# A graph network's gate pass: the next group's target columns and own products ahead of the present group's sums in TensorE's order

## The reference

```python
xs = x[src]
xd = x[dst]
att = jax.nn.sigmoid(xs @ W_att[:d] + xd @ W_att[d:] + b_att)
messages = (xs @ W_msg + b_msg) * att
aggregated = jax.ops.segment_sum(messages, dst, num_segments=num_nodes)
gi = aggregated @ W_ih.T + b_ih
gh = x @ W_hh.T + b_hh
```

## Time and profile before

| | |
|---|---|
| runs shown, median (lowest to highest) | 4062.01 us (4057.37 to 4065.38) |
| profiled execution | 4062.75 us |
| its span | 4060.9 us |
| TensorE matmul, weight load, busy | 3201.5 us (79%), 2287.2 us (56%) |
| VectorE, ScalarE, GpSimd, busy | 2351.6 (58%), 1235.2 (30%), 2712.1 us (67%) |
| TensorE's granted clock, mean over the span | 0.873 |

### The profile page before, as it was taken

How to read it: one execution, slowest core, us unless ns; L and a number is a source line. 1 busy time by engine, 2 the same in 40 slices (tenths; PEclk the granted TensorE clock), 3 DMA queues, 4 the chain that set the end, 5 groups by cost and what they waited for, 6 DMA issues and landing times. The chain is left out here.

```text
span 4060.9 us, 70549 instructions
## 1 busy us (share of the span) xinstructions
PE 3201.5 (79%) x23417; PEld 2287.2 (56%) x23529; DVE 2351.6 (58%) x7900; ACT 1235.2 (30%) x2830; POOL 2712.1 (67%) x2717
## 2 busy tenths in 40 slices
PE   4878888888778888835544449987999889997996
PEld 4766666766556565423322235545666666675554
DVE  6888888998656676666666752244233433333223
ACT  3433344445434454343322330003111221112112
POOL 4777777777527676457747747735777577774774
PEclk7999999999889998855555569998999999998998
DMA  5434445667825454123345469955999689996995
GB/s 153 118 83 105 108 112 113 140 128 147 187 88 138 126 142 121 33 65 79 83 95 105 89 150 294 295 174 187 305 300 300 202 274 303 304 301 204 296 294 183
DMA packets 529216, 702.83 MB, mean 173 GB/s; under 512 B 72345, under 2 KB 420648, under 8 KB 528084
## 3 DMA queue, kind: packets, MB, share of 16 engines
q1 hardware_dynamic: 421204, 436.31, 37.7%
q0 software_dynamic: 107648, 261.94, 23.5%
HBM read 579.27 MB, written 118.69 MB: 172 GB/s over the span
## 5 line engine op out<-in xcount | busy, mean ns | idle before, releaser
L1742 POOL DMA_INDIRECT pass_rows<-table_sage,src_idx x1040 | 1000.1, 962 | 352.4 <-issue 296.7
L1132 POOL DMA_INDIRECT first_rows<-table_tensor,src_idx x772 | 769.7, 997 | 248.4 <-issue 230.8
L1791 PE MATMUL pass_dense_ps<-x 128*128 128x512 f16 x3528 | 602.6, 327 | 30.2 <-DMA x<-table_sage 29.5
L2848 POOL DMA_INDIRECT sort_rows<-table_sort,slot_idx x392 | 398.1, 1016 | 170.6 <-issue 157.6
L1791 PE MATMUL pass_dense_ps<-rb 128*128 128x512 f16 x2646 | 466.3, 331 | 28.5 <-DMA rb<-table_sage 24.3
L1791 PEld LDWEIGHTS pass_dense_ps<-x 128*128 128x128 bf16 x3528 | 335.1, 98 | 242.6 <-DMA x<-table_sage 31.6
L1386 POOL DMA_INDIRECT pass_rows<-table_gate,src_idx x314 | 328.9, 1047 | 167.1 <-issue 90.5
L1791 PEld LDWEIGHTS pass_dense_ps<-rb 128*128 128x128 bf16 x2646 | 228.7, 98 | 234.7 <-DMA rb<-table_sage 23.8
L1870 DVE TENSOR_TENSOR pass_scaled_sums<-pass_sums_ps,rc 128x52 f32<-128x52 f32 (+16 forms) x316 | 56.9, 222 | 518.3 <-PE pass_sums_ps L1833 492.3
L1219 PE MATMUL pass_sums_ps<-pass_hot,pass_prod_a 128*128 128x128 f32 x1568 | 241.1, 301 | 142.2 <-DVE rb L1236 136.5
L1219 PEld LDWEIGHTS pass_sums_ps<-pass_hot,pass_prod_a 128*128 128x128 f32 x1568 | 208.5, 206 | 197.0 <-DVE rb L1236 182.0
(11 more groups left out here) (387 smaller groups left out, 6357.1 us busy)
## 6 DMA issues: line engine op xcount, KB each, us to landing
rb<-dense SPq DMA_DIRECT2D x196, 288.0 KB
x<-dense SPq DMA_DIRECT2D x294, 192.0 KB
x<-table_sage SPq DMA_DIRECT2D x294, 192.0 KB
rb<-dense SPq DMA_DIRECT2D x98, 309.5 KB
pass_counts<-dense SPq DMA_DIRECT2D x147, 192.0 KB
rb<-table_sage SPq DMA_DIRECT2D x294, 96.0 KB
dense<-re SPq DMA_DIRECT2D x49, 448.0 KB
dense<-x SPq DMA_DIRECT2D x42, 448.0 KB
```

Source lines behind the costliest of these rows:

```text
L1132: nc.gpsimd.indirect_dma_start(rows[:, h, t, :], None, table, bass.IndirectOffsetOnAxis(ap=idx[:, at:at + 1], axis=0)).then_inc(gathered[h ...
L1742: nc.gpsimd.indirect_dma_start(rows[:, h, t, :], None, table, bass.IndirectOffsetOnAxis(ap=idx[:, at:at + 1], axis=0)).then_inc(gathered[h ...
L1791: ins = nc.tensor.matmul(dense_ps[:, a * bank_cols + at:a * bank_cols + to], table_ring[:, k, from_table:from_table + P], counts_ring[:, k ...
L2848: nc.gpsimd.indirect_dma_start(rows[:, b, j, :], None, table, bass.IndirectOffsetOnAxis(ap=slot_idx[:, at:at + 1], axis=0)).then_inc(gathe ...
```

## The change

Target columns and own products of a group become a function, `columns_of(j)`, with the load of the bases in it. Group 0's are issued ahead of the loop. In the loop those of group j + 1 are issued after the dense steps of j and ahead of the sums of j; before, they were issued after the sums of j. The waits stay with their instructions.

```diff
-            at_dense_columns(0)
             starts = []
-            for j in range(COLD_GROUPS):
-                h, r = j % RING, j % 2
+
+            def columns_of(j):
+                nonlocal starts
                 if j % RING == 0:
                     starts = load_bases(PE_E, bases, 1 + HOT_GROUPS + j, min(RING, COLD_GROUPS - j))
                 at_dst(j, starts[j % RING])
                 for i in own_in[j]:
                     own_products(i)
+
+            at_dense_columns(0)
+            columns_of(0)
+            for j in range(COLD_GROUPS):
+                h, r = j % RING, j % 2
                 for n in steps_in[j]:
                     dense_step(n)
                     if n % BLOCKS == BLOCKS - 1 and n + 1 < STEPS:
                         at_dense_columns(n // BLOCKS + 1)
+                if j + 1 < COLD_GROUPS:
+                    columns_of(j + 1)
 
                 if j >= 2:
                     pe.wait_ge(added, j - 1)
```

## The result

The changed kernel takes 4024.31 us (median of 4 runs, 4022.41 to 4028.18), the kernel before 4061.55 us (4 runs, 4057.37 to 4065.38): a ratio of 0.9911, with a 95% interval of 0.9899 to 0.9922, some 36 us less. The forecast was 4028. The profiled execution took 4025.97 us with a span of 4024.1 us, against 4062.75 and 4060.9.

A forecast was written before the change was run, and what follows sets the result against it. It took the gate pass to be bound by waits: gathers from 1420 to 1540 us, the TensorE-ScalarE-VectorE chain elsewhere. Chain 58 us, gathers allow 34, the smaller decides: 4062.75 - 33.7 = 4029.0, so 4028 for the median, range 4016 to 4050.

The forecast's parts named there:

- The sum: Gate pass: the chain would give 58 us, the gathers allow 34; the smaller decides, so 33.7 us are won.
- Its deciding term: Gate pass on GpSimd: 314 gathers one behind the other limit the pass, leaving a gain of 33.7 us.
- The chain's term: TensorE to ScalarE to VectorE: one group's sums leave the way from columns to sigmoid, 43 x 1.35 = 58 us.
- The tail: End of the gate pass after the last gather: 1.73 us to land plus 5.66 us from last sigmoid to last sum.
- Sums held up behind the columns and own products: TensorE: each group's sums can be held up by 0.77 us; costed at nothing, 61 us without the cover of four groups.
- The 20 base loads: TensorE's sequencer: about 1.00 us each, now under the dense step; costed at nothing, 20 us if bare.
- a gather is longer where VectorE is denser: Gate pass stretches: gathers of 0.99 us with VectorE at 35.78 of 60, 1.074 us with 48.23 and 43.94.
- the bounds of 28 and 42 us: Gain the gathers allow: 28 us at the dearest stretch's 1.092 us per gather, 42 us at the mean of 1.047.
- the forecasts of waits and clock: Gate pass: VectorE's wait for sigmoids falls from 74.7 to under 25 us; TensorE's clock rises above 0.95.
- The clock that keeps its share: Rival: TensorE's clock stays at 0.91 over the gate pass, 22 us less, 4040; 0.26 together with a partly kept chain.
- The sigmoids that come no sooner: Rival: ScalarE's gates queued ahead hold the sigmoid in the gate pass, so nothing moves, 4062; chance 0.08.
- The clock that falls further: Rival: TensorE's clock in the gate pass drops to 0.82, 29 us more, 4091; decides from 0.87 downward; chance 0.06.

The follow-up runs named there:

- the freed pass: Gate pass of the changed order with 3 of 4 gathers per cold group, against the kernel before: ratio 0.9824, 3994.31 us; the pass 400.0 us long.
- that half of the move alone: Only the own products go ahead of the sums, target columns stay behind them, against the kernel before: ratio 0.9947, some 21.5 us.

## Why the prediction was right

**The sum held.** Its deciding term was the gathers: 314 x 1.074 + 95.8 = 433.0 us from the first to the end of the last, and a pass end at 1637.3. Measured: 335.1 + 93.6 + 1.8 = 430.5 us, mean 1.067, and 1637.63. The gain of 33.7 us in the pass came as 34.3. That the smaller of two limits decides is shown on the chip: taking gathers away wins 40 us in the new order and nothing in the old one, and adding 55.5 us to GpSimd adds 51.6 in the new one, 63.8 adds 21.2 in the old one.

**The chain's term.** The prediction gave the chain 58 us if nothing else were in the way. The pass with three gathers a group shows 476.4 us in the old order and 400.0 in the new, 76 us apart. The 58 came from VectorE's 43 waits at 1.35 us each; it did not count ScalarE's 144.7 us for the own products, nor what the clock gives back (0.96 in the freed pass, 0.91 in the kernel before). Which of the two makes up the 18 us was not tested. Since the gathers cap it, the miss cost nothing here.

**The tail** was put at 7.4 us (1.73 to land and 5.66 from the last sigmoid) and measured 9.3: the last sigmoid starts 1630.91 - 1628.37 = 2.54 us after the last gather, and the end comes 6.7 us behind it. Of these, 1.06 us are more than the 5.66 of before, and they lie ahead of VectorE's product at 1633.45. The addition and the one-hots in front of it begin at 1631.20, after 1.63 us of waiting for the sums, and so behind the sigmoid's start.

**Terms of nothing.** Sums held up behind the columns and own products cost nothing: GpSimd waits 1.8 us for them. The 20 base loads, moved under the dense step, kept their length (765/1000/1013 ns against the earlier trace rows).

**What failed: which limit held where.** The prediction had the gathers pace the old pass from 1420 to 1540 us, and the chain the rest. The old order with a quarter fewer gathers took as long in that stretch, 135.5 against 134.3 us, so the chain paced it too. That GpSimd hardly waits was taken for GpSimd setting the pace. The forecast used that stretch for its mean gather time, 1.074 us, and its pace happened to lie near that of the changed pass.

**What failed: why gathers get longer.** The step "a gather is longer where VectorE is denser" gave that mean. The size came out, the reason did not, and so the closeness of 34 to 34.3 us is partly luck; the bounds of 28 and 42 us did not need it. In the changed pass the stretch from 1300 to 1360 us has VectorE busy 40.52 and a mean of 46.84/44 = 1.065 us, that from 1480 to 1540 us has 45.76 and 46.23/46 = 1.005, and that from 1420 to 1480 us 44.39 and 46.95/43 = 1.092: no order. The pass with three gathers a group has VectorE busiest of all, 325.78 of 418 us, and the shortest mean, 1.037.

The upper bound of 42 us took the mean to stay at 1.047 us; it was 1.067, though VectorE runs the same instructions. What the traces show is that a gather's length goes with the single instruction under which it starts. Two weighings of the same size differ in where the gates lie: `pass_gates_apart` is on-chip memory (SBUF), `pass_gate_ps` is PSUM. From the changed kernel's timeline:

```profile
1390.52 0.95 DVE L1578 TENSOR_TENSOR pass_weighted<-pass_counts,pass_gate_ps 128x768 f32<-128x768 f16 x1
1390.75 0.94 POOL L1386 DMA_INDIRECT pass_rows<-table_gate,src_idx  x1 [0.30 <-issue]
...
1396.47 0.95 DVE L1578 TENSOR_TENSOR pass_weighted<-pass_counts,pass_gates_apart 128x768 f32<-128x768 f16 x1
1396.99 1.24 POOL L1386 DMA_INDIRECT pass_rows<-table_gate,src_idx  x1 [0.30 <-issue]
```

The first gather starts under a weighing with gates in PSUM and takes 0.94 us. The second starts under one with both operands in SBUF, takes 1.24 us and ends 0.81 us after it.

Counted over the pass, 53 gathers start under a weighing of the second kind, 48 of them take over 1.0 us, and each of the 48 ends 0.81 or 0.82 us after that weighing; under the first kind start 44, and none takes over 1.0. Over the traces of all twelve kernels it is 475 of 573 against 7 of 472. Gathers that start while VectorE builds one-hots run long as well: 43 of 46 take over 1.0 us. In the kernel before fewer gathers meet either: 41 start under a weighing of the second kind (35 of them over 1.0 us) and 38 under the building of one-hots (28). What the gathers under these two take beyond 0.945 us each sums to 34.5 us in the changed pass and 27.9 before, 6.6 more, and all gathers together grew by 6.2. The stretches fit too: from 1300 to 1360 us 10 of 44 gathers start under a weighing of the second kind, from 1480 to 1540 us 5 of 46. So the trace points to which instruction a gather meets, and how much of it is left, and not to VectorE's busy share. Why more gathers meet one in the changed pass is not shown, and no run moved the gates to test this.

**What failed: the forecasts of waits and clock.** VectorE's wait for the sigmoids was to fall under 25 us and fell from 74.7 to 44.4; the clock was to rise above 0.95 and rose to 0.93. Both assumed that the chain runs freely. It does in the pass with three gathers, where VectorE waits 16.5 us for the sigmoids and the clock is 0.96. With all gathers it is paced by them: ScalarE starts its sigmoids when the rows land (70.3 us of waiting that was not there before), VectorE waits behind ScalarE, and TensorE keeps idle pieces. The prediction did say that what comes late next is the gathers, but did not carry that wait through to the engines behind them.

**The rivals.** The clock that keeps its share (4040) would have left GpSimd waiting for the sums, and leaving TensorE work out would have helped; neither was so. The sigmoids that come no sooner (4062) fell with ScalarE's halved wait for the own products, and that half of the move alone is worth 21.5 us. The clock that falls further (4091) needed 0.87 and got 0.93.

## What to carry to other kernels

When an order on one engine lengthens a chain, work out the pace of the next limit before pricing the gain: here the chain gave up 76 us and the gathers let through 34. Count an engine's gaps between its instructions with its busy time, for GpSimd was busy 76% of the pass (335.1 of 439.8 us) and yet set its length. An engine that hardly waits need not set the pace: before the change GpSimd waited for the sums in 3.1 us of a stretch of 134, and a quarter fewer gathers left that stretch as long. And carry the new limit's wait through to every engine behind it before forecasting waits or clocks.

## What the runs showed of the hardware

- The gap of 0.305 us between two indirect gathers is not lost to GpSimd: a memset of 0.118 us in each of 314 gaps left the sum as it was (428.4 against 430.5 us), and one of 0.328 us cost 0.18 in the new order and 0.20 in the old one.
- Of the 53 gathers of the changed pass that started under a VectorE product of 128 x 768 with both operands in SBUF, 48 took over 1.0 us, against a median of 0.945, and ended 0.81 or 0.82 us after it. Of the 44 that started under the same product with one operand in PSUM, none took over 1.0 us.
- A gather's duration is far from constant, and few long ones make the mean. Minimum, median and maximum over the changed pass (then the first and last start) are

```profile
L1386 POOL DMA_INDIRECT pass_rows<-table_gate,src_idx x314: 940/945/1824, 1197.8 to 1627.4; - x157
```

so half of the gathers take 0.945 us or less and the mean is 1.067. A pass of 314 gathers at the median would be 314 x 0.122 = 38 us shorter in GpSimd's sum, as large as the gain of this change.
